# Distance attention: another order of its steps on TensorE and VectorE, with halved spreads

## The reference, cut to what matters

```python
q = (h @ Wq.T + bq).reshape(B, S, HEADS, HEAD_DIM)   # k, v likewise
scores = einsum('bqhd,bkhd->bhqk', q, k) / sqrt(HEAD_DIM)
pos_emb = dist_emb[MAX_POS - 1 + distance]
scores = scores + einsum('bqhd,qkd->bhqk', q, pos_emb)
scores = scores + einsum('bkhd,qkd->bhqk', k, pos_emb)
probs = softmax(scores, axis=-1)
ctx = einsum('bhqk,bkhd->bqhd', probs, v)
```

## Time and profile before

| | us |
|---|---|
| median of 3 runs | 4276.71 (4276.64 to 4277.81) |
| profiled execution | 4306.47 |
| its span | 4304.8 |
| distance attention within the span | 2642 to 3952 |

### The profile page before, as it was taken

One profiled execution on the slowest core, in us unless ns is written; L12 is line 12 of the kernel. 1 busy time (PEld: TensorE's weight loads), 2 busy tenths in 40 slices (PEclk: granted clock), 3 DMA queues, 4 the chain that ended last, 5 costly groups with the idle time before them and its releaser, 6 DMA issues. The chain is left out here.

```text
span 4304.8 us, 71162 instructions
## 1 busy us (share of the span) xinstructions
PE 3468.7 (81%) x27092; PEld 2140.7 (50%) x27092; DVE 3423.9 (80%) x4264; ACT 2884.7 (67%) x2433; POOL 1096.6 (25%) x871
## 2 busy tenths in 40 slices
PE   3799999999999999999658724887887887887890
PEld 2233333333333333333347713777777777776690
DVE  7899999999999999999375544767777777777662
ACT  3899999999999999999323313565565565564430
POOL 2111111112212121112003344224224224321245
PEclk8899999999999999999869956998999998998995
DMA  4100000000000000000311236012012012002022
GB/s 130 26 12 6 12 12 12 6 12 12 12 12 6 12 12 12 6 12 9 104 65 40 59 76 149 17 24 51 17 24 51 17 24 51 17 17 66 26 64 66
DMA packets 145095, 146.43 MB, mean 34 GB/s; under 512 B 62672, under 2 KB 123696, under 8 KB 140112
## 3 DMA queue, kind: packets, MB, share of 16 engines
q1 hardware_dynamic: 136144, 125.04, 12.0%
q0 software_dynamic: 8704, 17.84, 1.8%
HBM read 90.73 MB, written 52.10 MB: 33 GB/s over the span
## 5 line engine op out<-in xcount | busy, mean ns | idle before, releaser
L704 PE MATMUL psA<-wave,diag 128*128 128x512 f32 x3072 | 1443.9, 621 | 137.1 <-DVE score L860 86.8
L772 ACT ACTIVATE wave<-wave 128x2048 f32<-128x2048 int32 x640 | 1181.3, 1904 | 3.6 <-DVE wave L847 2.2
L704 PEld LDWEIGHTS psA<-wave,diag 128*128 128x128 f32 x3072 | 583.7, 197 | 897.3 <-issue 701.8
L641 POOL TENSOR_TENSOR diag<-ident,par 128x128 f32<-128x128 f32 x384 | 294.9, 794 | 1438.5 <-PE psA L704 1438.5
L822 DVE TENSOR_SCALAR wave<-s,par 128x2048 int32<-128x2048 int32 x480 | 615.0, 1281 | 0.0
L847 DVE TENSOR_SCALAR wave<-wave 128x2048 int32<-128x2048 int32 x512 | 611.6, 1221 | 0.0
L1716 POOL COPY kb<-ks 48x2048 bf16<-48x2048 bf16 x80 | 309.5, 3868 | 721.6 <-PE psR L1775 534.0
L1888 DVE TENSOR_TENSOR S<-psR,S 128x1024 f32<-128x1024 f32 x256 | 312.7, 1222 | 218.8 <-PE psR L1791 218.8
L1860 ACT ACTIVATE W<-psR 128x1024 f32<-128x1024 f32 x256 | 260.1, 1028 | 268.5 <-PE psR L1800 267.0
L1800 PE MATMUL psR<-ident,S 128*128 128x128 f32 x2048 | 297.9, 298 | 113.1 <-DVE S L1903 111.4
L737 ACT ACTIVATE s<-psS,par 128x1024 int32<-128x1024 f32 x256 | 282.8, 1105 | 132.1 <-PE psS L667 132.1
(11 more groups left out here) (258 smaller groups left out, 4485.9 us busy)
## 6 DMA issues: line engine op xcount, KB each, us to landing
ks<-kb_parts SPq DMA_DIRECT2D x56, 384.0 KB, 6.2
qs<-qb_parts SPq DMA_DIRECT2D x32, 384.0 KB, 6.2
ys<-f_ys SPq DMA_DIRECT2D x36, 256.0 KB
wave_out<-og SPq DMA_DIRECT2D x33, 256.0 KB, 2.1
o<-wave_out SPq DMA_DIRECT2D x8, 1024.0 KB, 5.2
qp<-qa_parts SPq DMA_DIRECT2D x32, 192.0 KB, 3.5
kp<-ka_parts SPq DMA_DIRECT2D x32, 192.0 KB, 4.0
f_wu<-in_w_up SPq DMA_DIRECT2D x2, 2048.0 KB, 9.4
```

Of the source, the lines that this page charges most:

```text
L641: ins = pool.tensor_tensor(diag[:, h % 2, f, :], ident[:], par[:, u, 1, h * NF + f:h * NF + f + 1] .to_broadcast((P, P)), ALU.mult)
L704: mm = pe.matmul(psA[:, kt, :], diag[:, h % 2, f, :], wave[:, h % 2, f, kt * L:(kt + 1) * L], start=(f == 0), stop=(f == PE_F - 1), skip_g ...
L772: act.activation(wave[:, h % 2, f, :], angle[:, h % 2, f, :], ACT.Sin, scale=float(TWO_PI / 2.0 ** 32)).then_inc(sine, 1)
```

## The change

It does five things. (1) A tile's first unit, the "head", moves behind the turned (last) unit of the tile ahead: while transposes of that tile still read S, the head's r2 goes to r1[:, 1] and its add reads its second operand there; the last two values steps and both outputs of the tile ahead lie in the head. ScalarE's copy of r1 for the unit behind the head waits until VectorE took all four content chunks of the head. (2) Mixed units go content, position, content, three positions. (3) In the turned unit all four r1 of the head come behind its first content chunk, and r2 come among the later transposes, one at a time. (4) VectorE has an own list, `dve_plan`. (5) Key blocks go back and forth over tiles without a turn at a change of group, ks and kb buffers are numbered anew for that (`ks_of`, `kb_of`), and every spread is cut into two halves of pairs, each of two copies, with TensorE waiting for each half.

```diff
     def tile_of(u):
         q, t = divmod(u, QT)
-        return t if (q % QT + q // QT) % 2 == 0 else QT - 1 - t
-    def with_scores(u, others):
-        out, each = [], len(others) // 4
-        for k in range(4):
-            out.append(("c", u, k))
-            out += others[k * each:(k + 1) * each]
-            if k:
-                out.append(("max", u, k - 1))
-        return out + [("max", u, 3)]
-    def tile_steps(q):
+        return t if q % 2 == 0 else QT - 1 - t
+    def ks_of(u):
+        return (0, 1, 2, 0)[tile_of(u)] if u // (QT * QT) % 2 == 0 else (2, 1, 0, 2)[tile_of(u)]
+    def kb_of(u):
+        return (tile_of(u) + u // (QT * QT)) % 2
+    def chunks(kind, u):
+    def unit_head(u, q):
+        c, r2 = chunks("c", u), chunks("r2", u + 1)
+        if q is None:
+            return [step for k in range(4) for step in (c[k], r2[k])] + chunks("r1", u + 1)
+        r1 = chunks("r1", u + 1)
+        return [c[0], ("pv", q, 6), r2[0], c[1], ("o", q, 0), r2[1], c[2], r2[2], c[3], r2[3], r1[0],
+                ("pv", q, 7), r1[1], r1[2], r1[3], ("o", q, 1)]
+    def unit_mixed(u):
+        c, r1, r2 = chunks("c", u), chunks("r1", u + 1), chunks("r2", u + 1)
+        return [c[0], r1[0], c[1], r1[1], r1[2], r1[3], c[2], r2[0], c[3], r2[1], r2[2], r2[3]]
+    def unit_turned(u, q):
+        c = chunks("c", u)
+        r1, r2 = (chunks("r1", u + 1), chunks("r2", u + 1)) if q + 1 < NQ else ([], [])
+        e = [("e", q, j) for j in range(NPAIR)]
+        v = [("pv", q, j) for j in range(NQUAD)]
+        return ([c[0]] + r1 + [c[1], e[0], e[1], c[2], e[2], e[3], v[0], e[4], e[5], v[1], c[3], e[6], e[7], v[2]] +
+                r2[0:1] + [e[8], e[9], v[3]] + r2[1:2] + [e[10], e[11], v[4]] + r2[2:3] + [e[12], e[13]] + r2[3:4] +
+                [v[5], e[14], e[15]])
+    plan = chunks("r1", 0) + chunks("r2", 0) + unit_head(0, None)
+    for q in range(NQ):
         u = q * QT
-        last = u + QT - 1
-        out = with_scores(u, [("r2", u + 1, k) for k in range(CH)])
-        for v in (u + 1, u + 2):
-            out += with_scores(v, [(kind, v + 1, k) for kind in ("r1", "r2") for k in range(CH)])
-        after = [u + QT, u + QT + 1] if q + 1 < NQ else []
-        early = [("r1", after[0], k) for k in range(CH)] if after else []
-        late = [("r1", after[1], k) for k in range(CH)] if after else []
-        out += [("c", last, 0), ("max", last, 0), ("sub", q, 0), ("sub", q, 1)]
-        for k in range(4):
-            if k < 3:
-                out += [("c", last, k + 1), ("max", last, k + 1)]
-            for j in range(4 * k, 4 * k + 4):
-                out.append(("e", q, j))
-                if j % 2 and j > LAG:
-                    out.append(("pv", q, j // 2 - LAG // 2))
-                if j + 2 < NPAIR:
-                    out.append(("sub", q, j + 2))
-                if j in (1, 3, 6, 8) and early:
-                    out.append(early.pop(0))
-                if j >= 10 and late:
-                    out.append(late.pop(0))
-                if j == NPAIR // 2 + LAG + 1:
-                    out.append(("o", q, 0))
-        final = [("r2", after[0], k) for k in range(CH)] if after else []
-        return out + final[0:1] + [("pv", q, NQUAD - 1)] + final[1:3] + [("o", q, 1)] + final[3:4]
-    plan = [(kind, u, k) for kind, u in (("r1", 0), ("r1", 1), ("r2", 0)) for k in range(CH)]
-    plan += [step for q in range(NQ) for step in tile_steps(q)]
-    fills = [step for step in plan if step[0] in ("r1", "r2", "c", "e", "o")]
+        plan += unit_mixed(u + 1) + unit_mixed(u + 2) + unit_turned(u + 3, q)
+        plan += unit_head(u + QT, q) if q + 1 < NQ else [("pv", q, 6), ("o", q, 0), ("pv", q, 7), ("o", q, 1)]
+    def dve_head(u, q):
+        a, x = chunks("add", u), chunks("max", u)
+        ctx = [("ctx", q, 0)] if q is not None else []
+        return [a[0], x[0], a[1], x[1]] + ctx + [a[2], a[3], x[2], x[3]]
+    def dve_mixed(u, ctx):
+        a, x = chunks("add", u), chunks("max", u)
+        return [a[0]] + ctx + [a[1], x[0], x[1], a[2], a[3], x[2], x[3]]
+    def dve_turned(u, q):
+        a, x = chunks("add", u), chunks("max", u)
+        s = [("sub", q, j) for j in range(NPAIR)]
+        return ([a[0], x[0], s[0], s[1], a[1], s[2], s[3], x[1], a[2], s[4], s[5], x[2], s[6], s[7], a[3],
+                 s[8], s[9], x[3]] + s[10:])
+    dve_plan = dve_head(0, None)
+    for q in range(NQ):
+        u = q * QT
+        dve_plan += dve_mixed(u + 1, [("ctx", q - 1, 1)] if q else []) + dve_mixed(u + 2, []) + dve_turned(u + 3, q)
+        dve_plan += dve_head(u + QT, q) if q + 1 < NQ else [("ctx", q, 0), ("ctx", q, 1)]
+    fills = [step for step in plan if step[0] != "pv"]
-    by_dve = {step: n + 1 for n, step in enumerate(s for s in fills if s[0] in ("c", "o"))}
+    taken_by_dve = {"add": "c", "ctx": "o"}
+    by_dve = {(taken_by_dve[kind], i, k): n + 1
+              for n, (kind, i, k) in enumerate(s for s in dve_plan if s[0] in taken_by_dve)}
...
     def spread_steps():
+        for kind, i in (("q", 0), ("k", 0), ("k", 1)):
+            yield kind, i
         for q in range(NQ):
-            if q == 0:
-                yield "q", 0
-                yield "k", 0
-                yield "k", 1
-            elif q % QT == 0:
-                yield "q", q
-                yield "k", q * QT + 1
-                yield "k", q * QT
-            for t in (2, 3):
-                yield "k", q * QT + t
-            if (q + 1) % QT and q + 1 < NQ:
+            u = q * QT
+            yield "k", u + 2
+            yield "k", u + 3
+            if q + 1 < NQ:
                 yield "q", q + 1
+                for v in (u + QT, u + QT + 1):
+                    if v in k_spreads:
+                        yield "k", v
...
-            def spread(dst, src, ready):
+            def spread(dst, src, half, ready):
+                pairs = slice(half * PAIRS // 2, (half + 1) * PAIRS // 2)
                 for odd in range(2):
                     rows = slice(odd * ODD, odd * ODD + NR)
                     pool.tensor_copy(
-                        dst[rows, :, odd, :],
-                        src[rows, :, :].rearrange("r h (n two) -> r n h two", two=2)[:, :, :, odd]
+                        dst[rows, pairs, odd, :],
+                        src[rows, :, :].rearrange("r h (n two) -> r n h two", two=2)[:, pairs, :, odd]
             def spread_q(q):
                 pool.wait_ge(qs_loaded[q % 2], 32 * (q // 2 + 1))
-                if q:
-                    pool.wait_ge(filled, fill["r1", q * QT - 1, CH - 1] + 1)
-                spread(qb, qs[:, q % 2, :, :], qb_ready)
+                for half in range(2):
+                    if q:
+                        pool.wait_ge(filled, fill["r1", q * QT - 1, 2 * half + 1] + 1)
+                    spread(qb, qs[:, q % 2, :, :], half, qb_ready)
...
-                spread(kb[:, kt % KB, :, :, :], ks[:, kt % KS, :, :], kb_ready)
+                for half in range(2):
+                    spread(kb[:, kb_of(u), :, :, :], ks[:, ks_of(u), :, :], half, kb_ready)
...
                 if kind == "r1":
                     src, way, w0 = qb, 1, L - 1 + P * kt - P * qt
-                    if k == 0:
-                        pe.wait_ge(qb_ready, 2 * (q + 1))
+                    if u % QT == 0 and k % 2 == 0:
+                        pe.wait_ge(qb_ready, 4 * q + k + 2)
                 else:
-                    src, way, w0 = kb[:, kt % KB, :, :, :], 0, L - 1 + P * qt - P * kt
-                    if k == 0 and u in k_spreads:
-                        pe.wait_ge(kb_ready, 2 * (k_order.index(u) + 1))
+                    src, way, w0 = kb[:, kb_of(u), :, :, :], 0, L - 1 + P * qt - P * kt
+                    if u in k_spreads and k % 2 == 0:
+                        pe.wait_ge(kb_ready, 4 * k_order.index(u) + k + 2)
...
-                dst = r1[:, u % 2, :, :] if kind == "r1" else S[:, :, kt * P:(kt + 1) * P]
+                if kind == "r1":
+                    if u % QT == 1:
+                        act.wait_ge(dve_took, by_dve["c", u - 1, 3])
+                    dst = r1[:, u % 2, :, :]
+                else:
+                    dst = r1[:, 1, :, :] if u % QT == 0 else S[:, :, kt * P:(kt + 1) * P]
...
-                part = S[:, k * HB:(k + 1) * HB, kt * P:(kt + 1) * P]
+                hs = slice(k * HB, (k + 1) * HB)
+                part = S[:, hs, kt * P:(kt + 1) * P]
+                second = r1[:, 1, hs, :] if u % QT == 0 else part
...
-                dve.tensor_tensor(part, psR[:, n % RING, :, :].rearrange("p a (h n) -> p (a h) n", n=P), part,
+                dve.tensor_tensor(part, psR[:, n % RING, :, :].rearrange("p a (h n) -> p (a h) n", n=P), second,
...
-            for kind, i, k in plan:
-                if kind == "c":
+            for kind, i, k in dve_plan:
+                if kind == "add":
```

(56 more changed lines are left out.)

4 lines of the change are left out of this document (1 added, 3 removed).

## The result

The changed kernel takes 4168.32 us (median), before 4276.68 us measured beside it: ratio 0.9744, 95% interval 0.9725 to 0.9763, so 108 us or 2.6% faster. (One of its four executions took 8820 us at full granted clock, unlike the others; the ratio is without it, and the median without it is 4166.32.) The profiled execution took 4163.56 us, that of before 4306.47, which is 30 us above the median of its kernel. Of these 143 us, 33 lie outside the stage, where the code is the same: GpSimd's first query spread starts at 2619.90 us where it started at 2641.28 (21.4), and what follows the last output is 12.0 shorter. From the first query spread to the last output it takes 1198.78 us (2619.90 to 3818.68) where it took 1308.44 (2641.28 to 3949.72): 109.7 less.

What follows compares the result with a forecast made beforehand. Bound: the ring of three psR slots and queue order, no engine full. Tiles 103, changes of group 10, start 6.2 and last tile 5.8 sum to 125 us off the profiled 4306.47: 4181, median 4153; range 4115 to 4212.

Steps and rivals of the forecast that it cites:

- The bound: Whole stage: three psR slots and queue order limit it; a fill waits until the fill three before was taken.
- Mixed units: Two units of a tile: 11.95 and 10.3 us, together 22.3 against 26.8 before.
- Turn and head: A tile's turned unit plus the next tile's first unit: 49.05 us together, before 51.4.
- A tile: One ordinary tile: 71.3 us against 78.15, 6.85 saved, 15 times: 103 us.
- rival (c): Turn: TensorE granted 1.2 GHz after close gaps, +16.6 us a tile, 250 in all: 4400 us; chance 0.04.
- Changes of group: Three changes: old 11.4 us excess goes, copies delay subtractions 8.5 us; total excess 35.5 to 25.5, 10 us saved.
- The bound of 15.4: Upper limit in us for one change of group: its spreads' whole length; lower limit 0, all hidden.
- Ends: Start of the stage 6.2 us saved, last tile 5.8 us saved.
- Sum: Whole kernel: 125 us off the profiled execution, giving 4181; median 4153 us.
- GpSimd's half copy: Each copy of 1024 in a spread: 1.93 us taken, 2.3 as bound, 2.2 estimated from the Trainium skill.
- Rival (b): Turn of every tile: query spread over 3 us late meets subtractions, up to 7.7 us a tile: 4245; chance 0.08.
- Rival (a): Turn and head lose their 2.35 us at slot handovers, only mixed units gain: 4188, or 4223; chance 0.20.

Runs made afterwards that it cites:

- the short spreads: Changed kernel with the two key spreads at each change of group copying only a sixteenth of their elements: 4131.5 us, 37 us less than the changed kernel.
- the kernel before with three positions: Kernel before with only the mixed units changed to content, position, content, three positions, maxima in pairs: 4213.72 us, ratio 0.9865.
- The weave: Changed kernel with the eight position chunks of the next tile's first unit put behind the turn's last transposes, not among them: 4251.63 us, 83 us more.
- halves: Changed kernel with every spread in two copies of 2048 again and readers waiting for the whole spread: 4180.2 us, 12 us more.
- VectorE's order: Changed kernel with VectorE's turned unit in groups again (add, maximum, subtractions): 4178.57 us, 10 us more.
- three positions: Changed kernel with mixed units back to two positions between contents and maxima one by one behind the adds: 4197.46 us, 29 us more.

## Why the prediction was right, point by point

- *The bound* (ring and queue order, no engine full): right. The same counts of instructions on TensorE, VectorE and ScalarE take 110 us less in the stage.
- *Mixed units* 11.95 and 10.3 us: measured 11.69 and 10.16. *Turn and head* 49.05: measured 33.45+15.13 = 48.6 (they carry 42 fills, not the 28 that the prediction names; no term used that count), with e4's 1.6 us wait measured as 1.53 and the first content behind the head released by ScalarE as said. A tile: 71.3 forecast, 70.43 measured; 7.7 saved in place of 6.85, which is 13 us more over 15 tiles.
- *The clock*: rival (c) did not happen in the turn; an ordinary tile has 1.00. But six of eleven ordinary distances are 71.4 to 72.6, 9 us in all, which no term held. They lie in the unit behind the head. There the clock falls behind waits of 0.55 and 1.11 us (0.60 from 3018.3 to 3026.8), and content and transposes then take 1.03 and 1.9 us for 0.6 and 1.04. Tiles of 70.43 have the same two waits (the content at 2794.98 above) and keep 1.00:

```profile
3018.38 0.62 PE L1808 MATMUL psR<-ks,qs 112*128 112x128 bf16 x8 [1.11 <-ACT r L1876]
3018.84 1.47 PE L1811 MATMUL psR<-ident,r 128*128 128x128 f32 x8
...
3022.11 1.03 PE L1808 MATMUL psR<-ks,qs 112*128 112x128 bf16 x8 [0.95 <-DVE ctxt L1942]
3022.94 1.91 PE L1811 MATMUL psR<-ident,r 128*128 128x128 f32 x8
```

- *Changes of group*: the mis-sized term. Forecast 10 us saved; measured 5.6 lost, a term wrong in its sign. Distances of 82.54, 85.07 and 82.99 less 3x70.43 are 39.3 us; before, 89.56 and the two others like it came to 33.7 over 3x78.15. The mechanism that makes the new excess was the forecast one, the short spreads show it. Too small was the price of one change: 8.5 us, where the three lost 12.1, 14.6 and 12.6, and the first turn alone 11.0 (44.5 us for 33.45). A half copy is 2.05 us and not 1.93; TensorE's slow chunks behind its longer waits had no place in the walk, nor had the stop of 1.66 us. The bound of 15.4 held. The old excess was read too narrowly: the prediction gave its 11.4 us to buffers that come free late, but TensorE waited for subtractions that met copies there as well.
- *Ends*: start 4.1 us saved of 6.2. The two units gave 4.9, but content of unit 1 began 35.8 us behind the first query spread, where 33.3 was forecast and before had 34.9: r1 waited for the transfer of T and not for the halved spread, and later position chunks waited 1.9, 2.1 and 3.1 us for GpSimd's key copies. Last tile 4.7 of 5.8.
- *Sum*: 100.9 us in the fifteen periods (forecast 113), 4.1 and 4.7 at the ends: 109.7 for 125. The miss is the changes of group (-15.6), the slow stretches (-9) and the ends (-3.2), less the 13 that tiles gave more. So the total is nearer than its terms: an error of 13 one way hid part of 28 the other. (The profiled execution, 4163.56, lies under the 4181 forecast for it because 33 us of its distance to that of before are outside the stage.)
- *GpSimd's half copy*: 1.93 was taken, 2.05 measured. The 2.2 us of the prediction's other estimate come from 2.6 cycles an element, which the Trainium skill (GPSIMD Engine Reference, Elementwise — side-by-side cycle accounting) gives for an operation with two inputs. A copy has one, so that it came near shows nothing.
- Rival (b): the query spread ended 2.0 us into the turn (2890.23 for a turn at about 2888.3), 0.8 later than walked and 2.4 ahead of the first subtraction; it was near but did not meet them. Rival (a) did not occur.

Left open: the split of the 45 us (49 in the stage) between the kernel before with three positions and the changed kernel. The weave (83), halves (12), VectorE's order (10) and three positions (29) were each taken from the changed kernel and don't add up, since they share waits. Neither the new numbering of key buffers nor the place of the head behind the turn was undone alone. Why some tiles have the slow stretch and others not, and what stops TensorE at the second change, isn't known.

## What to carry to other kernels

Where engines hand each other slots of a small ring, walk the queues with durations from the trace: here a walk of 66 fills was within 1.3% of the measured tile, as long as nothing met a GpSimd copy and the clock stayed up. Put ready work of the next stage behind the instruction that starts the wait, and give the engine that empties the ring an order of its own; then ask what each short operation behind a long one holds (moving one 0.9 us context ahead of an add was worth 26 us). Before moving a GpSimd copy, list VectorE's operations with two SBUF inputs in that stretch: they alternate with it one by one. Here six subtractions lost 8.7 us to eight copies, and a single one took 2.96 us for 1.22.

## What the runs showed of the hardware that was not expected

- A copy of 48x1024 took 2.0 to 2.07 us, one of 48x2048 3.8 to 3.9, one of 48x64 0.33: a fixed part of some 0.2 us in each. Four of these spread a tile in 8.24 us, two in 7.7.
- TensorE's clock fell behind a row of waits none of which passed 1.2 us (0.95 over a tile of 72.3 us), and stayed at 1.00 in tiles with the same waits ahead of the same chunks; which tiles it takes isn't settled by these runs.
- TensorE stopped for 1.7 to 3.6 us with no releaser in the profile, in eight of ten experiments and in both kernels, each time in the second change of group.
- Copy and subtraction slow each other: with eight copies beside six subtractions the subtractions lost 8.7 us, the copies 4.3.
